# The scan's result held with channels on partitions, in three buffers, and the ends of the last two sequences written in another order

## The reference

```python
x = x + mixer(layernorm(x))       # Mamba-2 block and a gated MLP
x = x + moe(layernorm(x))         # 8 experts, 2 per token

# inside mixer, per sequence, chunks of 128 tokens, 8 heads of 64 channels:
z, xBC, dt = split(rmsnorm(h) @ in_proj)
xs, B, C   = split(silu(causal_conv(xBC)))
y   = (C B^T * L) @ (xs * dt)               # within the chunk
y  += (C @ state) * exp(cumsum(dt * A))     # from the chunks before
y  += D_param * xs
y   = y * silu(z)
y   = y * rsqrt(mean(y^2) + 1e-6) * w       # over 512 channels
h1  = h + y @ out_proj
out = h1 + (silu(h2 @ gate) * (h2 @ up)) @ down,   h2 = rmsnorm(h1)
```

## Time and profile before

| | us |
|---|---|
| median of three runs | 725.72 (724.36 to 727.06) |
| the profiled execution's own time | 726.26 |
| its span, first to last instruction | 724.4 |
| PE busy | 692.7 (96%) |
| PE weight loads busy | 444.1 (61%) |
| DVE busy | 581.6 (80%) |
| ACT busy | 240.8 (33%) |
| POOL busy | 223.6 (31%) |

### The profile page before, as it was taken

How to read it: one execution, slowest core, us unless ns; L and a number is a source line. 1 busy time by engine, 2 the same in 40 slices (tenths; PEclk the granted TensorE clock), 3 DMA queues, 4 the chain that set the end, 5 groups by cost and what they waited for, 6 DMA issues and landing times.

```text
span 724.4 us, 10151 instructions
## 1 busy us (share of the span) xinstructions
PE 692.7 (96%) x2843; PEld 444.1 (61%) x2844; DVE 581.6 (80%) x1471; ACT 240.8 (33%) x487; POOL 223.6 (31%) x380
## 2 busy tenths in 40 slices
PE   5989999999999989999989999999999999999995
PEld 4457665558656766775865666666665555555563
DVE  3899999877866574476768888888888888988882
ACT  1576766585477435323121111111111111111110
POOL 2132322413221241220020333333333343434333
PEclk8999999999999999999999999999999999999999
DMA  9232002000220064033117891111151534434112
GB/s 317 64 117 89 30 1 85 34 1 1 70 106 0 1 210 153 1 92 120 33 51 253 278 300 29 26 27 28 29 178 34 149 64 122 97 90 130 30 22 30
DMA packets 39351, 63.22 MB, mean 87 GB/s; under 512 B 5456, under 2 KB 29072, under 8 KB 39312
## 3 DMA queue, kind: packets, MB, share of 16 engines
q1 hardware_dynamic: 31824, 52.61, 21.0%
q0 software_dynamic: 7488, 10.11, 8.8%
HBM read 52.88 MB, written 9.83 MB: 87 GB/s over the span
## 4 chain that ended last, share of the span: by engine, by line
PE 78%; DVE 11%; DMA 3%; issue 3%; ACT 2%; POOL 2%; POOLq 0%; DVEq 0%
PE ps L1110 23%; PE ps L1131 12%; PE ps L800 5%; PE ps L774 4%; PE ps L786 4%; PE ps L460 4%; PE ps L515 4%; PE ps L1119 3%; PE ps L582 3%; PE ps L639 3%; PE ps L529 3%; DMA out_rows<-big 2%; DVE big L1681 2%; DVE big L2313 2%; DVE big L1701 1%
## 5 line engine op out<-in xcount | busy, mean ns | idle before, releaser
L2313 DVE STREAM_TRANSPOSE big<-big 32x224 f32<-32x224 f32 x560 | 225.5, 403 | 8.4
L1110 PE MATMUL ps<-big 128*128 x512 | 198.6, 541 | 1.3 <-ACT big L1583 0.7
L1110 PEld LDWEIGHTS ps<-big 128*128 128x128 f32 x512 | 96.3, 190 | 88.0 <-issue 86.4
L1131 PE MATMUL ps<-big 128*128 x448 | 102.2, 380 | 1.0 <-DVE big L2313 0.6
L1589 ACT ACTIVATE big<-ps 128x896 f32<-128x896 f32 x36 | 33.0, 917 | 200.8 <-PE ps L1110 177.5
L1131 PEld LDWEIGHTS ps<-big 128*128 128x128 f32 x448 | 82.6, 190 | 11.7 <-issue 1.8
L2365 POOL TENSOR_TENSOR big<-big 128x1 f32<-128x1 f32 x110 | 22.0, 200 | 176.9 <-DVE big L2303 153.4
L460 PEld LDWEIGHTS ps<-big 128*128 128x128 f32 x319 | 39.9, 145 | 38.7 <-issue 27.6
L460 PE MATMUL ps<-big 128*128 128x128 f32 x319 | 52.4, 279 | 8.1 <-DVE big L1764 2.3
L2553 POOL DMA_INDIRECT out_rows<-big x32 | 51.3, 1603 | 18.2 <-issue 18.2
L1681 DVE SCALAR_TENSOR_TENSOR big<-ps,big 128x511 f32<-128x511 f32 (+2 forms) x72 | 53.0, 747 | 4.3 <-ACT big L1236 2.3
(11 more groups left out here) (246 smaller groups left out, 1019.7 us busy)
## 6 DMA issues: line engine op xcount, KB each, us to landing
big<-in_w SPq DMA_DIRECT2D x36, 896.0 KB, 7.8
big<-cum_rows SPq DMA_DIRECT2D x16, 512.0 KB, 5.7
out_rows<-big SPq DMA_DIRECT2D x4, 512.0 KB, 2.9
xn_rows<-big SPq DMA_DIRECT2D x4, 512.0 KB, 3.1
big<-in_hidden SPq DMA_DIRECT2D x1, 1536.0 KB, 12.3
big<-in_in_proj SPq DMA_DIRECT2D x1, 1288.0 KB, 7.1
big<-in_gate SPq DMA_DIRECT2D x1, 640.0 KB, 13.2
big<-in_up SPq DMA_DIRECT2D x1, 640.0 KB, 8.7
```

Source lines behind the costliest of these rows:

```text
L1110: last = mm(bank(bk + n)[:, 0:HALF], xT[:, k, :], expert_cols(e, off + k * M + n * HALF, HALF), start=(k == 0), stop=(k == KD - 1))
L1131: last = mm(bank(7)[:, 0:D], hTs[:, half, j * P:(j + 1) * P], expert_cols(e, 2 * KD * M + j * D, D), start=(j == 0), stop=(j == MB - 1))
L2313: last = V.transpose(hTs[c * SQ:(c + 1) * SQ, half, :].rearrange("p (j t) -> p j t", j=MB)[:, :, q * SQ:(q + 1) * SQ], ha[q * SQ:(q + 1) * ...
```

## The change

The result `y` of a chunk now has channels on partitions and tokens on columns, so that it can be the weights of `out_` as it stands. In detail:

- `z_` and `diag` swap their two operands; `diag` now writes each head to 64 partitions of DIAG, two heads side by side. `off_` becomes four products of 128 columns.
- `off` multiplies by `decb`, the decay of every channel and token, instead of `dec` over the heads. `decb` is filled by two new transfers for each sequence (`spread_heads`) and one new exponential of 128x1536 on ACT (`head_decay`).
- `x_D` reads the convolution's result directly: four instructions of 128 columns, with `D_param` per partition.
- `yT_` and `yT_copy` go. The sum of the squares now runs over partitions: ACT squares (`square_y`, no sum), POOL adds the four blocks in two instructions (`fold`), PE sums over the partitions with a product of one column (`sumsq`), ACT adds epsilon (`mean_y`), POOL takes the power (`scale_y`, one instruction instead of two).
- `yb` has three buffers; `off` and `y_` wait for `out_` and `square_y` of the chunk three before. `junk_y` has two. The banks' waits on `yT_taken` become waits on `mean_ready`.
- `y_` waits for all four `z_silu` of the sequence instead of its own.
- The orders of PE, DVE, ACT and POOL are changed at the end of sequences 2 and 3, and `WARM_LAST` goes from 8 to 2.

```diff
-WARM_START, WARM_LAST, WARM_PLACE, WARM_ROWS = 5, 8, 5, 6
+WARM_START, WARM_LAST, WARM_PLACE, WARM_ROWS = 5, 2, 5, 6
...
+            def spread_heads(n):
+                rows = cum_rows[(n * CH + 1) * HEADS:(n + 1) * CH * HEADS, :].rearrange("(q f) l -> f q l", f=2)
+                if n > 0:
+                    sp.wait_ge(off_scaled, n * (CH - 1))
+                for f in range(2):
+                    sp.dma_start(decb[f * HD:(f + 1) * HD, :, :].rearrange("p c (j l) -> p (c j) l", l=P),
+                                 rows[f:f + 1, :, :].to_broadcast([HD, (CH - 1) * HEADS // 2, P])).then_inc(decb_in, 16)
...
@@ def hT_(n)
-                    pe.wait_ge(yT_taken, nth(n - 2, CH, 2))
+                    pe.wait_ge(mean_ready, nth(n - 2, CH, 2))
@@ def z_(n, t)
-                    last = mm(bank(z_bank(n, t)), hT[:, k, t * P:(t + 1) * P], win[:, k, 0:INNER],
+                    last = mm(bank(z_bank(n, t)), win[:, k, t * P:(t + 1) * P], hT[:, k, :],
@@ def off_(n, c)
-                mm(bank(STATES), xc[n % 2][:, 5, l], st, start=True, stop=True).then_inc(off_ps, 1)
+                for j in range(4):
+                    q = slice(j * P, (j + 1) * P)
+                    last = mm(bank(STATES)[:, q], st[:, q], xc[n % 2][:, 5, l], start=True, stop=True)
+                last.then_inc(off_ps, 1)
@@ def diag(n, c)
-                    last = mm(bank(DIAG)[:, hh * HD:(hh + 1) * HD], em[n % 2][:, c, hh * P:(hh + 1) * P],
-                              xdt[:, c % 2, hh * HD:(hh + 1) * HD], start=True, stop=True)
+                    rows = slice(hh % 2 * HD, (hh % 2 + 1) * HD)
+                    last = mm(bank(DIAG)[rows, hh // 2 * P:(hh // 2 + 1) * P], xdt[:, c % 2, hh * HD:(hh + 1) * HD],
+                              em[n % 2][:, c, hh * P:(hh + 1) * P], start=True, stop=True)
@@ PE
+            def sumsq(n, c):
+                pe.wait_ge(folded, nth(n, CH, c))
...
+                mm(bank(TURN1)[:, 0:1], junk_y[:, c % 2, 0:P], cst[:, C_MEAN:C_MEAN + 1], start=True, stop=True).then_inc(ssy_ps, 1)
@@ def out_(n, c)
-                pe.wait_ge(yT_taken, nth(n, CH, c))
+                pe.wait_ge(y4_ready, nth(n, CH, c))
...
-                    last = mm(bank(MISC)[:, 0:D], yTs[:, k, :], wout[:, k, :], start=(k == 0), stop=(k == 3))
+                    last = mm(bank(MISC)[:, 0:D], yb[:, (n * CH + c) % 3, k * P:(k + 1) * P], wout[:, k, :], start=(k == 0), stop=(k == 3))
@@ order of PE, end of sequence 2
-            yT_(2, 3)
+            out_(2, 3)
+            sumsq(2, 3)
             mlp_down(1, 3)
             diag(3, 0)
-            out_(2, 3)
-            diag(3, 1)
             state_(3, 0)
             h2T_(2)
+            diag(3, 1)
             off_(3, 1)
-            yT_(3, 0)
             mlp_gate(2, 0)
             mlp_up(2, 0)
             xnT_(1, 0)
             out_(3, 0)
-            yT_(3, 1)
+            sumsq(3, 0)
             state_(3, 1)
             front(3, 2)
+            mlp_gate(2, 1)
             positions(0)
-            mlp_gate(2, 1)
@@ order of PE, end of sequence 3
             out_(3, 1)
+            sumsq(3, 1)
+            diag(3, 3)
             mlp_down(2, 0)
-            diag(3, 3)
             mlp_down(2, 1)
-            yT_(3, 2)
-            logits(1, 1)
-            mlp_down(2, 2)
+            sumsq(3, 2)
             out_(3, 2)
-            yT_(3, 3)
-            mlp_down(2, 3)
+            sumsq(3, 3)
+            mlp_down(2, 2)
             out_(3, 3)
+            mlp_down(2, 3)
+            logits(1, 1)
             keep_warm(DIAG, WARM_LAST)
             h2T_(3)
+            mlp_gate(3, 0)
+            mlp_up(3, 0)
             positions(1)
             xnT_(2, 0)
-            mlp_gate(3, 0)
-            mlp_up(3, 0)
             mlp_gate(3, 1)
@@ ACT
-                for hh in range(HEADS):
-                    q = slice(hh * HD, (hh + 1) * HD)
-                    last = A(xsd[:, c % 2, q], xs[:, q], ACT.Copy, scale=vec[:, V_D + hh:V_D + hh + 1])
+                for j in range(4):
+                    last = A(xsd[:, c % 2, j * P:(j + 1) * P], xc[n % 2][:, j, c * P:(c + 1) * P], ACT.Copy, scale=vec[:, V_D + j:V_D + j + 1])
+            def head_decay(n):
+                act.wait_ge(decb_in, 32 * (n + 1))
+                A(decb, decb, ACT.Exp).then_inc(decb_ready, 1)
...
-                A(junk_y, yb[:, c % 2, :], ACT.Square, accum_out=ssy[:, c:c + 1]).then_inc(ssy_ready, 1)
+                A(junk_y[:, c % 2, :], yb[:, (n * CH + c) % 3, :], ACT.Square).then_inc(square_ready, 1)
+            def mean_y(n, c):
+                act.wait_ge(ssy_ps, nth(n, CH, c))
...
+                A(vy[:, c:c + 1], bank(TURN1)[:, 0:1], ACT.Identity, bias=cst[:, C_EPS:C_EPS + 1]).then_inc(mean_ready, 1)
@@ order of ACT, sequence 2 (in the others alike)
+            square_y(2, 3)
             square_h(2, 2)
-            yT_copy(2, 3)
-            square_y(2, 3)
+            mean_y(2, 3)
             square_h(2, 3)
             x_D(3, 1)
             decay(3, 3)
+            head_decay(3)
             h2T0(2)
@@ DVE, def off(n, c)
-                if n * CH + c >= 2:
-                    v.wait_ge(yT_taken, n * CH + c - 1)
-                    v.wait_ge(ssy_ready, n * CH + c - 1)
-                V.tensor_tensor(heads(yb[:, c % 2, :]), heads(bank(STATES)), over_head(dec[n % 2][:, 1, c, :]), ALU.mult).then_inc(off_scaled, 1)
+                if n * CH + c >= 3:
+                    v.wait_ge(o_ps, n * CH + c - 2)
+                    v.wait_ge(square_ready, n * CH + c - 2)
+                v.wait_ge(decb_ready, n + 1)
+                V.tensor_tensor(yb[:, (n * CH + c) % 3, :], bank(STATES), decb[:, c - 1, :], ALU.mult).then_inc(off_scaled, 1)
@@ order of DVE, end of sequence 2
             add_mlp(1, 2)
-            route_next(0)
+            h1_(2, 3)
             add_mlp(1, 3)
+            h2(2)
             ln2_stats(1)
             y_(3, 0)
-            h1_(2, 3)
-            xn_(1)
-            h2(2)
             state(3, 0)
             h2T1(2)
+            xn_(1)
+            route_next(0)
             scores(3, 2)
@@ order of DVE, end of sequence 3
             h1_(3, 1)
             add_mlp(2, 0)
-            route_pick(1)
             h1_(3, 2)
+            add_mlp(2, 1)
             route_rec(0)
-            add_mlp(2, 1)
+            h1_(3, 3)
             add_mlp(2, 2)
+            h2(3)
             add_mlp(2, 3)
             ln2_stats(2)
-            h1_(3, 3)
+            h2T1(3)
+            route_pick(1)
+            xn_(2)
             route_next(1)
-            h2(3)
-            xn_(2)
-            h2T1(3)
             route_place(0)
@@ POOL
+            def fold(n, c):
+                q = junk_y[:, c % 2, :]
+                g.wait_ge(square_ready, nth(n, CH, c))
+                G.tensor_tensor(q[:, 0:2 * P], q[:, 0:2 * P], q[:, 2 * P:4 * P], ALU.add).then_inc(fold_step, 1)
+                g.wait_ge(fold_step, nth(n, CH, c))
+                G.tensor_tensor(q[:, 0:P], q[:, 0:P], q[:, P:2 * P], ALU.add).then_inc(folded, 1)
             def scale_y(n, c):
-                G.tensor_scalar(vy[:, c:c + 1], ssy[:, c:c + 1], 1.0 / INNER, RMS_EPS, ALU.mult, ALU.add).then_inc(pool_ry, 1)
                 G.tensor_tensor(ry[:, c:c + 1], vy[:, c:c + 1], half[:, 0:1], ALU.pow).then_inc(ry_ready, 1)
```

More of the change, by code:

```diff
@@ L407, in _ @@
             store_xn(0)
+            spread_heads(3)
             store_x1(1)
@@ L849, in _ @@
             out_(0, 0)
+            sumsq(0, 0)
             xbc_(1, 5)
@@ L863, in _ @@
             out_(0, 1)
-            yT_(0, 2)
+            sumsq(0, 1)
             diag(0, 3)
             out_(0, 2)
+            sumsq(0, 2)
             hT_(2)
@@ L897, in _ @@
             out_(1, 0)
+            sumsq(1, 0)
             z_(2, 3)
@@ L912, in _ @@
             out_(1, 1)
-            yT_(1, 2)
+            sumsq(1, 1)
             mlp_up(0, 3)
@@ L916, in _ @@
             mlp_gate(0, 4)
+            sumsq(1, 2)
             mlp_up(0, 4)
@@ L925, in _ @@
             front(2, 0)
-            yT_(1, 3)
             dt_(3)
@@ L935, in _ @@
             out_(1, 3)
+            sumsq(1, 3)
             xbc_(3, 1)
@@ L957, in _ @@
             out_(2, 0)
+            sumsq(2, 0)
             mlp_gate(1, 1)
             diag(2, 2)
-            yT_(2, 1)
             mlp_up(1, 1)
@@ L967, in _ @@
             out_(2, 1)
+            sumsq(2, 1)
             mlp_up(1, 2)
@@ L982, in _ @@
             out_(2, 2)
+            sumsq(2, 2)
             mlp_down(1, 0)
@@ L1371, in _ @@
             decay(0, 3)
+            head_decay(0)
             front(0, 1)
@@ L1425, in _ @@
             decay(1, 3)
+            head_decay(1)
             square_h(0, 2)
@@ L1468, in _ @@
             front(2, 0)
-            yT_copy(1, 3)
             square_y(1, 3)
             dt_e(3)
+            head_decay(2)
             x_D(2, 0)
@@ L1549, in _ @@
             gate(2, 4)
+            x_D(3, 3)
             xnT_copy(1, 1)
@@ L1552, in _ @@
             gate(2, 5)
```

(33 more changed lines are left out.)

201 lines of the change are left out of this document (96 added, 105 removed).

## The result

The changed kernel takes 718.13 us (median of 4 runs, 713.94 to 719.16), the kernel before on the same chip 725.04 us (723.27 to 727.06): a ratio of 0.990, 95% interval 0.987 to 0.9931. A second series gave 717.63 against 725.18 us (0.9897, 0.9875 to 0.9918). The profiled execution took 719.16 us with a span of 717.4, against 726.26 and 724.4 before: 7.0 us less in the span, where the sum of the prediction had 11.4.

A forecast was written before the change was run, and what follows sets the result against it. DVE bounds the first phase up to 139 us, PE from there to 243.4 us. The terms -3.8 - 5.6 - 0.8 - 2.5 + 1.3 sum to -11.4 us, giving 714.3 us; 8 in 10 range some 708 to 722.

The forecast's parts named there:

- the stall that stays: Rival, chance 0.13: PE still stalls at `h2T_(2)` because the factor comes late; 3.4 of 5.6 us missing, 717.7 us.
- `diag`: PE, 16 records per `diag`: 1.16 us instead of 1.73, a gain of 0.57 each, taken as 0.55.
- The first rival, no overlap: Split products of `diag` do not run beside each other, 2.03 us each instead of 1.16: 721.3 us, chance 0.14.
- The rule's 719 us: Tiling-mode changes drain TensorE; at 0.87 us each, eight counted `diag` give 0 instead of -4.6: about 719 us.
- `sumsq`: PE, per chunk: 0.22 us for the one-column product in place of 0.44 for four transposes, a gain of 0.2.
- End of sequence 2: PE up to `mlp_gate(2, 0)`: 261.8 us instead of 267.4, -5.6, from wait, low clock, `yT_` and two `diag`.
- End of sequence 3: PE from 298.44 us to `mlp_gate(3, 2)`: -2.5; work up to the second `out_` summed to 12.9, wait about 1.4.
- PE waits for `fold`: Rival, chance 0.15: `sumsq` waits in PE's queue behind ACT and POOL, four waits cost 13.6 us, 727.9 us.
- DVE may not ... I take +1.3 us: DVE loses time beside POOL's added folds: 0.9 us in the stretch DVE bounds, 0.4 at the ends; bounds 0 and 4.
- Up to `mlp_down(2, 0)`: PE, after `mlp_gate(2, 0)`: one `diag` and one `yT_` more are saved, -0.8 us.
- ACT nothing: ACT's changed work, including the new `head_decay` exponential of 1.48 us, costs nothing because ACT's idle time hides it.
- 194.6 to 243.4: Stretch where PE is the bound: three `diag` and three `yT_` gain 2.3 us.

The follow-up runs named there:

- orders-alone kernel: Kernel before, old layout and two buffers, with the changed orders at the ends of sequences 2 and 3 and two keep-warm rounds: 724.76 us, ratio 0.9999.
- grouped heads: Changed kernel with the heads of `diag` in the order 0, 2, 4, 6, 1, 3, 5, 7: 720.82 us.
- layout alone: Changed kernel with the old orders at the ends of sequences 2 and 3 (two exceptions) and eight keep-warm rounds: 731.12 us, ratio 1.0077.
- kernel with two buffers: Changed kernel with two buffers for the scan's result instead of three: 717.77 us.
- two orders kernel: Changed kernel with `gate(2, 0)` before `square_y(3, 1)` on ACT and `hidden_(3, 0)` before `slots(0)` on DVE: 713.62 us, ratio 0.9842.

## Why the prediction came out as it did

The sign and the range (708 to 722) were right. The forecast of 714.3 was 3.8 us too low, and the median lies outside the 711 to 717 that had the chance of 0.46. The nearest number among the rivals is the 717.7 of the stall that stays, and that stall is gone: such a nearness tells nothing.

*The working, redone*: the parts named for -5.6 add up to 5.9, and those for 12.9 to 12.8; neither moves the forecast by more than 0.3 us.

*`diag`*: right in kind, and a little too dear. It takes 1.02 us. What stands behind it takes longer than in the kernel before: by 0.14 us at `state_(3, 0)` (257.99 - 256.93 = 1.06 us, where the orders-alone kernel shows 0.92), which would give the 1.16 of the forecast, but by 0.05 us at `mlp_gate(2, 2)` (1.82 for 1.77), and by as much behind most of the others. So a `diag` costs 1.07 us as a rule, and gains 0.66 instead of 0.55. The first rival, no overlap, falls with the 1.02 us and the grouped heads. The Trainium skill ("TensorEngine Tiling (Array Packing)", Tiling Modes) has the engine drain at each change of the mode. The 0.05 to 0.14 us don't speak against that, but no run here shows that they are a drain. The rule's 719 us did not come, since the changes are far from 0.87 us dear.

*`sumsq`*: right. It holds PE for 0.14 us, and the instruction behind it takes some 0.08 more (`xbc_(1, 5)` 1.80 for 1.71): 0.22. *`head_decay`*: 1.47 us for 1.48, and its transfers 5.9 us for 5; PE never waits for either.

*End of sequence 2*: right, -5.5 for -5.6, no stall, clock 1.00 at `h2T_(2)`, transposes 1.09 us instead of 1.96. The rival of the stall that stays falls. I had ascribed these 5.6 us to steps that can be added up. They can't: in this stretch the orders alone are worth 1.4 us and the layout alone 1.9, and over the whole the orders alone gain nothing and the layout alone costs 5.9 us (731.12 - 725.18).

*End of sequence 3*: -2.6 for -2.5, with 0.95 us of wait where I had 1.4 and another of 0.89 before `mlp_gate(3, 0)`.

*PE waits for `fold`*: it never does. But the sum costs in another way: it moves other work.

*The step that failed first*: "DVE may not ... I take +1.3 us". The kernel with two buffers, whose start is near that of the kernel before (15.92 against 16.09), is 2.2 us later at `diag(1, 2)` relative to its start, where 0.9 was forecast, and 2.1 us later at `mlp_gate(0, 2)`; by the prediction's own sign (over 2 us either way) this part is wrong. The 2.2 is not sharp: against the orders-alone kernel (start 16.25) it is 2.9. The part that is the same in all these profiles is the 1.35 us between `diag(0, 3)` and `diag(1, 2)`, and that alone is over 0.9. I priced the time that POOL works more (and `fold` too low: 0.72 and 0.52 us at 84.77 us, for 0.61 and 0.35). What counted was where POOL's old instructions fall. The Trainium skill ("GPSIMD Engine Reference", Key points) names two kinds of victims, and the trace has both: `apart` 3.22 against 4.88 us, and `scores`, with two SBUF inputs, 1.22 against 2.00 to 2.30 (the 2.30 at 81.61 us after the change, where the kernel before has 1.22 at 80.45). The prediction said that the rows show only the first kind; the earlier trace rows did, but the row of `scores(1, 0)` at 95.98 us, 2.00 against the 1.22 of others, was there to be read.

*Up to `mlp_down(2, 0)`*: +0.9 for -0.8. I looked at what goes from PE and not at ACT's order, where `square_y(3, 1)` had moved ahead of `gate(2, 0)`. The two orders kernel gets 1.2 of it back. "ACT nothing" is what failed: the cover was idle time on average, while the waits were in its order. *194.6 to 243.4*: -1.6 for -2.3; 0.42 us are two new waits for `conv_taps`, at 200.92 and 203.14 us. With the measured 0.66 and 0.22 us the three `diag` and `yT_` should even have brought 2.6, so 0.6 stays open.

*Start and clock*: the sum had nothing for the +1.4 at the start and the +0.8 between `mlp_gate(3, 2)` and the second expert tile. The changed instructions don't bring them of necessity, but both profiles of the changed kernel have both. The +0.8 is 1.7 in the first expert tile less 1.0 in the routing ahead of it, where it is the kernel before whose clock falls (16.52 us for 15.52 from `raw_turn(0)` to `choose`). In the first tile the clock was 0.64 after the change, and 1.00 in the kernel with two orders, for the same eight records; of fourteen profiles four have the long tile, all with the new layout, and the kernel before hasn't:

```profile
368.53 4.96 PE L1117 MATMUL ps<-big 128*128 x8 [0.67 <-ACT big L1598]
...
368.50:373.30 4.80, 4.77 (x8) 2.34 (x9) 0.54 (x6) 1.08 (x1) 1.49 (x4) 0.64 0.10 28
```
```profile
364.32 3.27 PE L1117 MATMUL ps<-big 128*128 x8 [0.67 <-ACT big L1598]
...
364.30:367.40 3.10, 3.08 (x8) 1.63 (x9) 0.61 (x6) 1.07 (x1) 1.50 (x4) 1.00 0.04 7
```
